# Second FFN of a four-layer block: gate and up of the routed slots as three products of rounded parts

## The reference, cut to what matters

```python
x = x + _L0_xattn_ref(...)     # a selective scan over 2 x 512 tokens
x = x + _L0_ffn_ref(...)       # 32 experts, 8 of them a token
x = x + _L1_xattn_ref(...)     # attention: 16 heads, 256 keys
x = x + _L1_ffn_ref(...)       # the layer that the change is in

def _L1_ffn_ref(x, centroids, gate_bias, wg_s, wu_s, wd_s, wg, wu, wd):
    def _swiglu(x, wg, wu, wd):
        return jax.nn.silu(x @ wg) * (x @ wu) @ wd
    shared = _swiglu(x, wg_s, wu_s, wd_s) * RATIO
    affinity = jax.nn.sigmoid(jnp.einsum('bsh,eh->bse', x, centroids))
    _, top_idx = jax.lax.top_k(affinity + gate_bias, K)      # K = 2 of 16
    ...
    for e in range(E):                                       # H = 256, I = 128
        routed = routed + mask[..., e:e + 1] * _swiglu(x, wg[e], wu[e], wd[e])
    return shared + routed
```

## Time and profile before

| | |
|---|---|
| median of 3 runs | 692.14 us (691.43 to 693.7) |
| profiled execution | 690.36 us |
| its span, first to last instruction | 688.6 us |
| mean granted PE clock | 0.98 |
| PE / PEld / DVE / ACT / POOL busy | 91% / 74% / 71% / 56% / 40% |

### The profile page before, as it was taken

One profiled execution on the slowest core, in us unless ns is written; L12 is line 12 of the kernel. 1 busy time (PEld: TensorE's weight loads), 2 busy tenths in 40 slices (PEclk: granted clock), 3 DMA queues, 4 the chain that ended last, 5 costly groups with the idle time before them and its releaser, 6 DMA issues.

```text
span 688.6 us, 10769 instructions
## 1 busy us (share of the span) xinstructions
PE 625.7 (91%) x3640; PEld 511.1 (74%) x3640; DVE 488.7 (71%) x1034; ACT 385.8 (56%) x790; POOL 275.2 (40%) x280
## 2 busy tenths in 40 slices
PE   7657759999999999999979999999999999999894
PEld 2346535554677888888868999999899988778773
DVE  5999999999976565446456766668577865654365
ACT  4866667644146546445367777777876765423221
POOL 1356610002144444445444655655455861241204
PEclk9789999999999999999999999999999999999998
DMA  6677844665645354444229232242111221355524
GB/s 194 200 270 265 278 156 149 204 204 178 182 130 173 104 177 124 154 153 150 79 90 339 96 135 79 83 147 78 32 31 47 78 78 47 123 171 166 181 96 122
DMA packets 58134, 98.89 MB, mean 144 GB/s; under 512 B 7000, under 2 KB 26976, under 8 KB 58080
## 3 DMA queue, kind: packets, MB, share of 16 engines
q1 hardware_dynamic: 56544, 94.00, 43.0%
q0 software_dynamic: 1536, 4.20, 1.9%
HBM read 78.51 MB, written 19.66 MB: 143 GB/s over the span
## 4 chain that ended last, share of the span: by engine, by line
PE 58%; DVE 26%; issue 7%; ACT 6%; another core or an unknown queue 1%; POOL 1%; DMA 0%; DVEq 0%; SPq 0%; ACTq 0%; POOLq 0%
PE bank L97 15%; PE bank L98 14%; PE bank L99 14%; DVE state L1432 10%; PE bank L884 5%; DVE read_out L1442 4%; PE bank L822 3%; PE bank L905 2%; ACT probs L1262 2%; PE bank L873 2%; ACT bank L1015 1%; DVE u_sb L1358 1%; DVE x_tok L1456 1%; DVE bank L1697 1%
## 5 line engine op out<-in xcount | busy, mean ns | idle before, releaser
L1994 POOL TENSOR_TENSOR w_lo<-w_raw,w_hi 128x768 fp32r<-128x768 f32 (+1 forms) x70 | 112.5, 1609 | 171.7 <-ACT w_hi L979 169.4
L97 PE MATMUL bank<-xt_hi,w_hi 128*128 128x512 f32 x224 | 91.1, 406 | 1.3 <-DVE hidden_lo L1349 1.3
L98 PE MATMUL bank<-xt_lo,w_hi 128*128 128x512 f32 x224 | 88.7, 396 | 0.0
L99 PE MATMUL bank<-xt_hi,w_lo 128*128 128x512 f32 x224 | 88.5, 395 | 0.0
L979 ACT ACTIVATE w_hi<-w_raw 128x768 fp32r<-128x768 f32 (+1 forms) x70 | 52.1, 745 | 58.4 <-PE bank L99 46.4
L1262 ACT ACTIVATE probs<-scores,row_min 128x256 f32<-128x256 f32 x128 | 63.8, 501 | 18.7 <-DVE row_min L1825 18.5
L2101 POOL TENSOR_TENSOR probs<-probs,row_scale 128x512 f32<-128x512 f32 x64 | 66.6, 1040 | 5.0
L1825 DVE CUSTOM_DVE_ANT_0 scores<-bank,mask_bias 128x256 f32<-128x256 f32 x128 | 48.8, 419 | 18.7 <-PE bank L99 18.7
L979 ACT ACTIVATE probs_t_hi<-bank 128x512 fp32r<-128x512 f32 x64 | 38.2, 598 | 36.8 <-PE bank L822 36.1
L510 PEld LDWEIGHTS bank<-identity,read_out 128*128 128x128 f32 x272 | 34.4, 153 | 30.8 <-DVE read_out L1442 17.9
L1130 ACT ACTIVATE gated<-bank 128x512 f32<-128x512 f32 x52 | 31.1, 597 | 42.1 <-PE bank L604 26.9
(11 more groups left out here) (233 smaller groups left out, 1747.0 us busy)
## 6 DMA issues: line engine op xcount, KB each, us to landing
w_raw<-in_ffn_w SPq DMA_DIRECT2D x38, 384.0 KB, 3.5
b_rows<-bc_scratch SPq DMA_DIRECT2D x32, 256.0 KB, 4.9
c_rows<-bc_scratch SPq DMA_DIRECT2D x32, 256.0 KB, 4.0
w_raw<-fold_scratch SPq DMA_DIRECT2D x32, 256.0 KB, 2.9
experts<-in_ffn_w SPq DMA_DIRECT2D x16, 384.0 KB, 4.2
route_bc<-route_scratch SPq DMA_DIRECT2D x31, 192.0 KB, 3.4
slots_scratch<-nothing SPq DMA_DIRECT2D x2, 2944.0 KB, 13.2
slots_in<-slots_scratch SPq DMA_DIRECT2D x22, 256.0 KB
```

What stands on the lines that cost most here:

```text
L97: e.matmul(out, w_hi, m_hi, start=first, stop=False)
L98: e.matmul(out, w_hi, m_lo, start=False, stop=False)
L99: return e.matmul(out, w_lo, m_hi, start=False, stop=last)
L1994: e.tensor_tensor(lo[:, 0:n], w_raw[(p - WHOLE) % RAW][:, 0:n], hi[:, 0:n].bitcast(F32), ALU.subtract).then_inc(sem("w_lo"), 1)
```

## The change

Gate and up of the slots' blocks become `product3` of rounded parts. The slots are split in each round (ACT rounds bank 0 into `slots_hi`, DVE subtracts into `slots_lo`), and PE's `turn_slots` and `gate_up_slots` now wait for `slots_lo`. The gate and up weights of the 16 experts are split once: `round_expert` on ACT, `rest_expert` on POOL, both on 128 x 512 elements. Experts 0 to 3 are done in attention units 17, 21, 25 and 29, experts 4 to 7 in units 60 to 63, and two experts in each of the units 64 to 67. `lo` is written over the loaded weights, and the first four experts are loaded into the last slots of the table, so `find_expert_of` has one more DVE instruction to number them so. The tiles of the two shared units get other places, and some semaphores are merged.

```diff
+        FIRST_EXPERTS = 4
+        experts_split_at = {17 + 4 * x: (x,) for x in range(FIRST_EXPERTS)}
+        experts_split_at.update({HEAD_UNITS - 4 + x: (FIRST_EXPERTS + x,) for x in range(4)})
+        experts_split_at.update({HEAD_UNITS + x: (8 + 2 * x, 9 + 2 * x) for x in range(4)})
...
@@ tensor: turn_slots, gate_up_slots
-                ps = take(0, ("slots_t", r + 1))
+                ps = take(0, ("slots_lo", r + 1))
...
-                at.wait_ge("ld_experts", 16 * E1)
-                at.wait_ge("slots_t", r + 1)
+                h, pair = half_and_pair(r)
+                at.wait_ge("experts_lo", E1 if h > 0 else min(E1, 2 * pair + 2))
+                at.wait_ge("slots_lo", r + 1)
                 ps = take(4 + r % 2, ("slots_hid", r + 1))
                 for j in range(blocks_in(r)):
                     for w in range(WH):
-                        last = e.matmul(ps[:, j * WIDTH:(j + 1) * WIDTH].rearrange("p (k i) -> p k i", k=2),
-                                        slots_t[r % 2][:, w, j * P:(j + 1) * P],
-                                        experts[:, bass.ds(expert[r, j] * 3, 2), w * P:(w + 1) * P],
-                                        start=w == 0, stop=w == WH - 1)
+                        cut = slice(j * P, (j + 1) * P)
+                        last = product3(e, ps[:, j * WIDTH:(j + 1) * WIDTH].rearrange("p (k i) -> p k i", k=2),
+                                        slots_hi[r % 2][:, w, cut], slots_lo[r % 2][:, w, cut],
+                                        experts_hi[:, bass.ds(expert[r, j] * 2, 2), w * P:(w + 1) * P],
+                                        experts_lo[:, bass.ds(expert[r, j] * 3, 2), w * P:(w + 1) * P],
+                                        w == 0, w == WH - 1)
@@ scalar
-                copy(slots_t[r % 2][:, :, 0:n], bank[0]..., "slots_t")
+                copy(slots_hi[r % 2][:, :, 0:n], bank[0]..., "slots_hi")
+            def round_expert(x):
...
+                n = expert_slot(x)
+                copy(experts_hi[:, 2 * n:2 * n + 2, :], experts[:, 3 * n:3 * n + 2, :], "experts_hi")
...
+                for x in experts_split_at.get(i, ()):
+                    round_expert(x)
@@ vector
+            def rest_slots(r):
...
+                split_rest(slots_lo[r % 2][:, :, 0:n], bank[0]..., slots_hi[r % 2][:, :, 0:n], "slots_lo")
...
+                if HEAD_UNITS <= i <= HEAD_UNITS + 2:
+                    rest_slots(i - HEAD_UNITS)
                 if i == HEAD_UNITS + 2:
                     multiply_slots(0)
...
+                if r > 1:
+                    rest_slots(r + 1)
                 multiply_slots(r)
@@ gpsimd
+            def rest_expert(x):
+                n = expert_slot(x)
+                at.wait_ge("experts_hi", x + 1)
+                e.tensor_tensor(experts_lo[:, 3 * n:3 * n + 2, :], experts[:, 3 * n:3 * n + 2, :],
+                                experts_hi[:, 2 * n:2 * n + 2, :].bitcast(F32), ALU.subtract)...
...
+                for x in experts_split_at.get(i, ()):
+                    rest_expert(x)
```

More of the change, by code:

```diff
@@ L234, in build @@
         experts_end = top[0]
+        top[0] = region_of["experts"]
+        experts_lo = place("experts_lo", [P, E1 * 3, WIDTH], F32R)
+        top[0] = region_of["route_bc3"] + 4 * HT - 4 * E1 * 2 * WIDTH
+        assert top[0] >= region_of["w2_lo"] and region_of["gated0"] == top[0] + 4 * 4 * 2 * WIDTH
+        experts_hi = place("experts_hi", [P, E1 * 2, WIDTH], F32R)
+        assert top[0] == shared_region
         top[0] = region_of["xt_whole"]
@@ L261, in build @@
         top[0] = region_of["mask_bias"]
-        slots_t = [place(f"slots_t{i}", [P, WH, 2 * P]) for i in range(2)]
+        slots_hi = [place(f"slots_hi{i}", [P, WH, 2 * P], F32R) for i in range(2)]
         slots_out = [place(f"slots_out{i}", [P, 2, WIDTH]) for i in range(3)]
+        assert top[0] <= region_of["scores0"]
+        top[0] = region_of["scores0"]
+        slots_lo = [place(f"slots_lo{i}", [P, WH, 2 * P], F32R) for i in range(2)]
         back = [place(f"back{i}", [P, WIDTH]) for i in range(TOP1 * HC)]
+        shared_hidden = [split_pair(f"shared_hidden{i}", [P, HT]) for i in range(3)]
+        shared_gated = [place("shared_gated0", [P, HT])]
         assert top[0] <= attention_end
+        top[0] = region_of["slots_out2"] + 4 * 2 * WIDTH
+        shared_gated.append(place("shared_gated1", [P, HT]))
+        assert top[0] <= region_of["scores0"]
         top[0] = max(attention_end, experts_end)
@@ L512, in y_sum @@
                                             stop=n == DS - 1 and l + c == 2)
-                last.then_inc(sem(f"y_sum{h}"), 1)
+                last.then_inc(sem("y_sum"), 1)
             def turn_z(h):
@@ L613, in down_whole @@
                     b = acc_banks(4)[i]
-                    ps = take(b, (f"acc_copy{i}", 1)) if first else bank[b]
+                    ps = take(b, ("acc_copy", 2)) if first else bank[b]
                     last = e.matmul(ps[:, :], w[:, 2 * WIDTH + i * P:2 * WIDTH + (i + 1) * P], hidden_whole[u % 3][:, :],
@@ L1095, in copy_acc @@
                 at.wait_ge(*finished(k))
-                copy(acc_sb[:, 0, :], bank[acc_banks(k)[0]][:, :], "acc_copy0")
+                copy(acc_sb[:, 0, :], bank[acc_banks(k)[0]][:, :], "acc_copy")
             def normalise_x(k, chunks=range(HC)):
@@ L1129, in activate_gate @@
                     at.wait_ge("hid", u - 1)
-                e.activation(gated[u % 2][:, :], bank[gate_up_banks(u)[0]][:, :], ACT.Silu).then_inc(sem("silu"), 1)
+                e.activation(gated_of(u)[:, :], bank[gate_up_banks(u)[0]][:, :], ACT.Silu).then_inc(sem("silu"), 1)
             def round_hidden(u):
@@ L1136, in round_hidden @@
                 at.wait_ge("down", u - 2)
-                copy(hidden_split[u % 3][0][:, :], bank[gate_up_banks(u)[1]][:, :], "hid_hi")
+                copy(hidden_of(u)[0][:, :], bank[gate_up_banks(u)[1]][:, :], "hid_hi")
             def fold_copy_turned(g):
@@ L1839, in rest_head @@
                     split_rest(lo[:, :], bank[7][:, :], hi[:, :], "head_lo")
+            def rest_slots(r):
+                if r >= ROUNDS:
+                    return
+                n = blocks_in(r) * P
+                at.wait_ge("slots_hi", r + 1)
+                split_rest(slots_lo[r % 2][:, :, 0:n], bank[0][:, :].rearrange("p (w s) -> p w s", w=WH)[:, :, 0:n],
+                           slots_hi[r % 2][:, :, 0:n], "slots_lo")
             def multiply_slots(r):
```

72 lines of the change are left out of this document (48 added, 24 removed).

## The result

| | before | after |
|---|---|---|
| median | 693.7 us (5 runs, 691.43 to 694.76) | 698.8 us (5 runs, 697.88 to 701.56) |
| ratio, 95% interval | | 1.008 (1.0055 to 1.0105) |
| profiled execution / its span | 690.36 / 688.6 us | 698.8 / 696.7 us |
| mean granted PE clock | 0.98 | 0.966 |

The changed kernel is slower by 0.8% in these runs, and the time lies above the predicted range. The first comparison is of rounds: the start of each `turn_slots` on PE, 24 of them in each trace, and the end of the span. "First turn to turn 4" is the time from the first to the fifth; turns are counted from 0, and turn 12 is the second half's first.

The account below looks back on a forecast made before the run. PE's array was taken to bound the rounds, its sequencer drawing level after the change. Terms +0.3 - 0.6 - 0.7 - 1.0 - 0.4 = -2.4 us gave 688.0 against the profiled 690.36, or 689.7 by medians; range 685.8 to 696.

Parts of the forecast that it names:

- the bound that the prediction names for a stall that costs nothing: Rounds 6 to 8, at ACT's 2.3 us stall: their gain is kept, -0.9 us, where the forecast took it as lost.
- Products: Gate-up rounds on PE: 12 products 0.12 us apart, 1.44 us a round, replace 4 float32 matmuls of 1.73.
- Addresses: PE's sequencer in gate-up: 8 address instructions a round instead of 4, 184 in all, each added one costing 0.132 us.
- rival (b): `gate_up_slots`, rounds 4 to 21: sequencer takes over with 12 addresses a round, +2 to +6 us, middle 696.1; chance 0.20.
- Round length: L873 to L873 in rounds 13 to 20: forecast 3.0 to 3.28 us, against 3.25 before.
- the middle, 3.14: Second half, rounds 12 to 21: round length taken between 2.99 and 3.28 us, giving -0.11 x 9 = -1.0 us.
- Start: Rounds 0 to 3 together, own gains included: +0.3 us, bounds -1.0 to +1.5.
- Attention: Attention before the rounds: its length should not change by more than 0.5 us.
- Tail: The stretch after the last rounds: no change.
- The step that failed: Rounds 6 to 8: ACT's 2.3 us stall has its end fixed by POOL's indirect DMAs, so the 0.9 us gain is lost.
- one round lies in the stall: Second half's rounds 12 to 21: one round lies in the 5.3 us stall at 638.9, so only 9 gain 0.11.

Follow-up runs that it names:

- experiment 1: Kernel before and changed kernel, both unedited, in another session, without stalls: 688.64 us before, 685.67 us changed, ratio 0.9946.
- experiment 2: Plain DMAs for POOL's indirect ones: without stalls 0.9996 (kernel before), 0.9947 (changed kernel); with stalls 0.9949, 0.991, beside the unedited kernel before at 694.46 us.
- experiment 3: With stalls, against the kernel before: changed kernel unedited 1.0059 (700.82 us); without its subtraction 1.0049; one product a part 1.0112; no range check 1.0386.
- experiments 3 and 5: Changed kernel with stalls: subtraction left out 1.0049, one float32 product a part 1.0112; in the later experiment, shared unit's up and down products moved later, 1.0076.
- before_spaced: Kernel before with POOL's first-half gathers spread over rounds 14 to 20, in a session without stalls: 1.0001 of the kernel before.
- paused scatters: Changed kernel with spread gathers and the second half's last four scatters behind round 9's turn: 0.9975 and 0.9976 of the kernel before, no stalls.

## Why the prediction was wrong

**What was right.** Without the stalls the sum comes out near, in part by luck. Its forecast of -2.4 us stands against -3.3 us from the first turn to the end between the profiled executions of experiment 1, and -3.5 of the medians:

| turns | forecast | no stalls (experiment 1) | stalls (before of experiment 2, after of 3) |
|---|---|---|---|
| 0 to 4 | +0.3 | +0.9 | +1.0 |
| 4 to 6 | -0.6 | -0.9 | -1.0 |
| 6 to 9 | 0 | -0.9 | -0.9 |
| 9 to 12 | -0.7 | -0.8 | **+5.3** |
| 12 to 22 | -1.0 | +0.3 | +1.0 |
| 22 to end | -0.4 | -1.9 | -1.4 |

With the gain of turns 6 to 9 kept, which is the bound that the prediction names for a stall that costs nothing, the forecast is -3.3 as well. But its other terms miss by +0.6, -0.3, -0.1, +1.3 and -1.5 us, and only together come to nothing.

*Products*: 0.12 apart, 1.42 us a round. *Addresses*: 184, rival (b)'s 276 did not come. *Round length* without stalls: 2.96 to 3.11 in turns 13 to 16, 3.77 from 16 to 17, where one read takes 0.97 us and 0.65 us of issue stand ahead of the turn, 3.07 to 3.39 in turns 17 to 22, and 2.96 for the one that reads no number. So the sequencer is the bound there as forecast, but at the upper end of 3.0 to 3.28 or above: the middle, 3.14, was the wrong choice, and turns 12 to 22 gain nothing. *Start*: +0.9 within its bounds of -1.0 to +1.5; without the subtraction (experiment 3) turns 0 to 4 take 13.66 us, less than the 14.1 of before, so the +0.9 is the wait for `slots_lo`. And the second half's chain was hardly moved: L1986, now L2050, comes at 586.46, 0.1 later than the first turn's shift explains. *Attention*: unmoved; from its first turn of probs to turn 0 it is 215.8 us in both profiles of the first comparison. *Tail*: a term put at nothing was worth some 1.3 us without stalls: DVE waited 1.87 us for the last gather and now 0.56.

**The step that failed** is that of the stalls: "I take their ends as fixed by these DMAs, so the gain is lost (bound: kept, -0.9)". The ends are indeed fixed. PE's last held signals came 11.4 us after POOL's first scatter in the kernel before (615.57 against 604.13, experiment 2) and 11.5 after it in the changed kernel (617.36 against 605.86, experiment 3). But a fixed end doesn't bound the cost. In that time the kernel before had made turn 10 (at 614.85), and the changed one had not: it made it at 620.25, since the signals of the `turn_hid` and the `down_slots` behind turn 8, and of turn 9 itself, were let through one at a time, at 611.60, 614.48 and 617.42. The stretch from turn 9 to 12 is 1.3 us longer with stalls than without for the kernel before (12.28 against 10.97) and 7.4 longer for the changed one (17.60 against 10.19). The term was sized as a gain of 0.9 lost, or kept. Measured, the gain of turns 6 to 9 was kept (-0.9) even with stalls, and the next stretch lost 6.1 us more than in the kernel before: +5.3 where the stretch gains 0.8 without stalls. These two profiles are of two sessions; within one, the first comparison, it is +4.5.

A part of the loss is PE's clock, which the sum held at full speed. The first stall and what follows, first the changed kernel of experiment 3, then the kernel before of experiment 2:

```profile
615.00:620.00 5.00, 1.13 (x4) 0.68 (x4) 2.07 (x4) 1.36 (x3) 0.75 (x1) 0.78 0.41 131
620.00:624.00 4.00, 3.75 (x18) 3.78 (x19) 2.05 (x5) 0.67 (x2) 0.00 (x0) 0.50 0.40 125
```
```profile
614.00:620.00 6.00, 5.13 (x28) 4.24 (x28) 2.80 (x6) 2.23 (x5) 0.14 (x1) 1.00 0.32 104
```

PE idles some 4 us and comes back at 1.2 GHz; the round then takes 4.97 us instead of 2.96, so 2.0 of the 7.4 us are the clock. The kernel before had work in between and stayed at 1.00. Its own second stall is long enough to lose the clock too (0.58 in 648 to 652 us), and there the two kernels lose nearly the same: turns 17 to 20 take 4.9 us more than without stalls before, 6.1 after. In the first comparison the kernel before kept its clock there and lost 3.0 us against the changed kernel's 5.7. The prediction had put nothing for this stall ("one round lies in the stall").

**What the forecast left out** besides: that a trace is of one session. The kernel before took 685 to 692 us in sessions without stalls and 691 to 700 in those with them, and only the rows "remote" of the earlier trace rows say which kind its trace is of; profiles without stalls have none in the rounds. The 3.1 us ahead of the rounds lie within the spread from execution to execution and were no part of any step.

**What stays open.** Why PE's signals are held from the fourth scatter on in the changed kernel (the signal of the `turn_hid` behind turn 8, due 3.8 us after the first scatter by experiment 1, came 1.9 late) and only from 7 us on, the sixth, in the kernel before. It is not the products, nor the subtraction, nor the shared unit (experiments 3 and 5), nor POOL's timing against the rounds: with one product a part turn 8 came 1.88 us after the first scatter, as in the kernel before, and the stall was long all the same. Left are what these kernels share: the places of the tiles, the merged semaphores, the experts' splits, the longer address table. No kernel tried has only one of them. Why plain DMAs with the same packets do no harm, and what differs between the sessions, is open as well; so is the change's worth beside a kernel before with spread gathers where there are stalls, for `before_spaced` met none.

## What to carry over

Before a change is costed, look for waits that no visible instruction ends. If there are any, run the unchanged kernel in a second session first: a stall that only some sessions show can turn the sign of a change of half a per cent, 0.9946 in one and 1.008 in the other here. A stall with a fixed end is no sink for a gain alone; price it in both directions, by how many dependent signals must pass while it lasts, and with the clock that PE loses when it idles. Keep indirect DMAs of POOL apart from one another where their results are not due: that gave back about 4 us where there were stalls, judged across sessions.

## What the runs showed of the hardware

- In the first comparison and in three of six sessions PE's semaphore updates reach ACT and DVE up to 6 us late while a run of eight indirect DMAs is worked off (5.78 us from 644.46 in the kernel after). DVE's signal of `slots_out`, given at 613.80 in the middle of the first stall, is seen by SP at 613.83 and by PE at 613.96. The DMA engines are not slow: the 128 completion packets of the second half's scatters start between 2.0 and 11.0 to 12.0 us after the first issue with stalls, and between 2.0 and 11.1 to 11.3 without (paused scatters left out). But of the 128 arrivals at the semaphore the traces hold 128 where there are no stalls, and 24 to 40 where there are. The first half's scatters, 2.5 to 4.7 us apart, have 128 of 128 everywhere.
- The Trainium skill (NOTIFIC — the notification-queue block, Overflow: three behaviours, one of which stalls the engine) says that the internal pipeline of the block that writes notification records always applies back-pressure rather than lose a record inside it. By it a crowd of records could hold back what makes them, which would fit the late signals and would not explain the missing records. No run here can show it, since every execution of this case, timed ones too, has its spans and clocks recorded.
- Where PE's sequencer is the bound, its instructions stand 0.07 to 0.08 us apart beside their own durations (3.33 us for 18 a round, 4.90 for 34), so 16 more cost 0.10 us each. A range check left out at the read comes back at each address: 16 more instructions a round, 22 us in all.
- 12 products of 256 columns with two-piece moving operands start 0.118 us apart, as contiguous ones do.
